# Values of a window attention evacuated flat and spread by DMA instead of by small engine operations

## The reference, in short

```
x = x + window_attention(gn(x))     # 8x8 windows, 16 heads of 16 channels
x = x + lif(gn(x) @ W.T + b)        # leaky integrate and fire over the 8 samples

qkv  = part @ qkv_w.T + qkv_b       # part: (windows, 64 tokens, 256)
attn = softmax(q*SCALE @ k.T + bias_table[...] + shift mask)
out  = attn @ v                     # per window and head: 64x64 times 64x16
```

## Time and profile before

| | |
|---|---|
| median of 3 runs | 576.61 us (572.59 to 577.72) |
| the profiled execution | 574.5 us, its span 572.8 us |
| TensorE (PE) busy | 470.8 us, 82% of the span |
| VectorE (DVE) busy | 464.0 us, 81% |
| ScalarE (ACT) busy | 434.2 us, 76% |
| GpSimd (POOL) busy | 318.1 us, 56% |
| DMA queue of SyncE | 91808 packets, 85.49 MB, 55.8% of 16 DMA engines' span |
| mean granted TensorE clock | 0.951 |

### The profile page before, as it was taken

How to read it: one execution, slowest core, us unless ns; L and a number is a source line. 1 busy time by engine, 2 the same in 40 slices (tenths; PEclk the granted TensorE clock), 3 DMA queues, 4 the chain that set the end, 5 groups by cost and what they waited for, 6 DMA issues and landing times.

```text
span 572.8 us, 18181 instructions
## 1 busy us (share of the span) xinstructions
PE 470.8 (82%) x6632; PEld 426.5 (74%) x6632; DVE 464.0 (81%) x995; ACT 434.2 (76%) x1045; POOL 318.1 (56%) x411
## 2 busy tenths in 40 slices
PE   0364699898999899899989998998999778599880
PEld 0364588787888788788878887887888667599770
DVE  6855568888898789888888987898778775779997
ACT  2275679888898899888888988998889567579830
POOL 6133365566555666655566656566555466867630
PEclk9978799999999999999999999999999898889975
DMA  6266066666777677666667776765565450221233
GB/s 185 73 171 160 15 168 173 175 167 181 190 200 192 165 189 180 165 174 170 181 168 196 193 190 167 186 153 150 155 154 153 132 148 3 92 75 74 97 116 137
DMA packets 92577, 86.09 MB, mean 150 GB/s; under 512 B 41842, under 2 KB 63604, under 8 KB 92532
## 3 DMA queue, kind: packets, MB, share of 16 engines
q1 hardware_dynamic: 91808, 85.49, 55.8%
q10 hardware_dynamic: 724, 0.01, 0.1%
HBM read 47.72 MB, written 33.55 MB: 142 GB/s over the span
## 4 chain that ended last, share of the span: by engine, by line
issue 26%; POOL 24%; PE 21%; DVE 11%; ACT 8%; DMA 6%; SPq 2%; POOLq 1%; ACTq 1%; DVEq 0%
POOL p_lo L426 11%; POOL xc L413 5%; POOL xn_lo L386 3%; DVE xc L865 3%; PE pv_ps L1009 3%; DMA k_stack<-k_spill1lo 2%; ACT v_hi L508 2%; DMA k_spill1lo<-k_lo 2%; PE proj_ps L909 2%; PE proj_ps L911 2%; PE proj_ps L910 2%; PE score_ps L986 2%; DVE charged L857 2%; DMA probs<-in_qkv_b_dram 1%; PE max_ps L953 1%
## 5 line engine op out<-in xcount | busy, mean ns | idle before, releaser
L426 POOL TENSOR_TENSOR p_lo<-probs,p_hi 128x512 f16<-128x512 f32 x128 | 146.7, 1167 | 162.6 <-ACT p_hi L587 162.6
L909 PE MATMUL proj_ps<-xn_hi,w_hi 128*128 128x256 f32 x288 | 86.1, 299 | 14.6 <-POOL xn_lo L386 14.0
L763 DVE TENSOR_TENSOR v_lo<-proj_ps,v_hi 64x128 f16<-64x128 f32 x256 | 74.1, 289 | 22.5 <-ACT v_hi L508 19.8
L586 ACT ACTIVATE probs<-score_ps 128x512 f32<-128x512 f32 x128 | 76.9, 601 | 18.1 <-PE score_ps L986 17.3
L976 PE MATMUL score_ps<-both_parts,bias_k 128*128 128x64 f16 x1024 | 82.6, 194 | 6.2 <-DMA k_stack<-k_spill1lo 4.3
L910 PE MATMUL proj_ps<-xn_lo,w_hi 128*128 128x256 f32 x288 | 83.1, 288 | 0.0
L911 PE MATMUL proj_ps<-xn_hi,w_lo 128*128 128x256 f32 x288 | 83.0, 288 | 0.0
L770 DVE TENSOR_REDUCE neg_max<-max_ps 128x16 f16<-128x1024 f32 x64 | 78.4, 1225 | 4.7 <-PE max_ps L959 2.7
L386 POOL TENSOR_TENSOR xn_lo<-xn,xn_hi 128x512 fp32r<-128x512 f32 x48 | 62.5, 1302 | 34.8 <-ACT xn_hi L480 34.7
L978 PE MATMUL score_ps<-q_stack,k_stack 96*128 96x64 f16 x1024 | 81.8, 193 | 0.0
L472 ACT ACTIVATE xn<-xc,shift,rstd 128x256 f32 (+1 forms) x128 | 70.6, 611 | 12.9 <-DVE shift L238 6.6
(11 more groups left out here) (144 smaller groups left out, 1434.9 us busy)
## 6 DMA issues: line engine op xcount, KB each, us to landing
xc<-in_x_dram SPq DMA_DIRECT2D x32, 256.0 KB, 4.9
k_stack<-k_spill0hi SPq DMA_DIRECT2D x32, 256.0 KB, 4.2
k_stack<-k_spill1hi SPq DMA_DIRECT2D x32, 256.0 KB, 4.1
out_dram<-xc SPq DMA_DIRECT2D x32, 256.0 KB, 2.3
q_hi<-q_flat SPq DMA_DIRECT2D x128, 32.0 KB, 2.0
k_spill0hi<-k_hi SPq DMA_DIRECT2D x16, 256.0 KB, 2.2
k_spill0lo<-k_lo SPq DMA_DIRECT2D x16, 256.0 KB, 2.4
q_stack<-q_spill0hi SPq DMA_DIRECT2D x32, 128.0 KB, 2.8
```

The lines of the kernel that those rows point to most:

```text
L426: pool.tensor_tensor(p_lo[p][:, quads, :, :].rearrange("p g w i -> p (g w i)"), probs[:, quads, :, :].rearrange("p g w i -> p (g w i)"), p ...
L586: act.activation(probs[:, quads, :, :].rearrange("p g w i -> p (g w i)"), score_ps[:, h, :], ACT.Exp)
L909: pe.matmul(dst, w_hi[:, c, cols], high[:, tok], start=(c == 0 and bias is None), stop=False)
```

## The change

The values are copied out of PSUM flat: one operation of 128 x 512 on ScalarE (high part) and one on VectorE (low part), into one tile `v_flat` (partition = token of two windows; part, tile, 256 channels). Four transfers per row, issued by SyncE behind `move_q_and_k`, put them into `v_all`, one for each window and each parity of head: 64 partitions, 4 runs of 256 bytes each. There are two such buffers, zeroed once, with the column of ones set once. For the runs to be contiguous the value columns of the weights are reordered at the start: even heads first, then odd ones, and within them channel by channel with the 8 heads innermost. The part shown for ScalarE's high part of the weights has its like on VectorE for the low part. `weigh_values` now reads its moving operand with a step of 8 elements of 2 bytes between neighbouring columns; before, 34 neighbouring elements were contiguous. `weigh_values` waits for the transfers (`v_moved`), and `v_high` waits until those of the row before have left `v_flat`. The second `v_high` behind `max_rows` is gone. `membrane` shares the space of `q_flat`, which is no longer used by then. Zeroing all value buffers is GpSimd's work now; half of it was VectorE's.

```diff
-        v_hi = [sb(f"v_hi{i}", [128, HALVES, 2, QUADS, 2, D + 1], f16) for i in range(4)]
-        v_lo = [sb(f"v_lo{i}", [128, HALVES, 2, QUADS, 2, D + 1], f16) for i in range(4)]
+        v_flat = sb("v_flat", [128, 2, 2, C], f16)
+        v_all = [sb(f"v_all{i}", [128, 2, 2, 2, 2, D + 1, 2 * QUADS], f16) for i in range(2)]
...
-        membrane = sb("membrane", [128, HALVES * ROWTOK], f32)
+        membrane = q_flat[:, :, :].rearrange("p t n -> p (t n)").bitcast(f32)
...
-        W_SCALES = ((0, C, QK_SCALE), (C, 3 * C, 1.0), (3 * C, OUTS, 1.0 / TAU))
+        W_SCALES = ((0, C, QK_SCALE), (C, 2 * C, 1.0), (3 * C, OUTS, 1.0 / TAU))
...
+        def v_weights(tile, order, c, e):
+            return tile[:, c, 2 * C:3 * C].rearrange(f"p ({order}) -> p e d n", e=2, d=D, n=2 * QUADS)[:, e, :, :]
+        AS_LOADED, BY_PARITY = "n e d", "e d n"
...
+            def move_v(slot, row):
+                sp.wait_ge(v_lo_done, row + 1)
+                for w in range(2):
+                    for e in range(2):
+                        sp.dma_start(v_all[slot][e * WS:(e + 1) * WS, :, :, w, e, 0:D, :].rearrange("j t p d n -> j (t p) (d n)"),
+                                     v_flat[w * WS:(w + 1) * WS, :, :, e * 128:(e + 1) * 128].rearrange("j t p c -> j (t p) c"))\
+                          .then_inc(v_moved[slot], 16)
...
                 if k % 2 == 0 and not is_last_row(row):
                     move_q_and_k((k // 2 + 1) % 2, row + 1, k // 2 + 1)
+                    move_v((k // 2 + 1) % 2, row + 1)
...
-            def v_high(slot, done, w):
+            def v_high(slot, done, moved=0):
                 act.wait_ge(v_ps_done, done)
-                for p in range(2):
-                    for e in range(2):
-                        last = act.activation(v_hi[2 * slot + p][e * WS:(e + 1) * WS, :, w, :, e, 0:D],
-                                              v_part(p, w, e), ACT.Copy)
-                last.then_inc(v_hi_done, 1)
+                wait(act, v_moved[1 - slot], moved)
+                act.activation(v_flat[:, 0, :, :].rearrange("t p c -> t (p c)"), proj_ps[:, 0, :], ACT.Copy).then_inc(v_hi_done, 1)
...
+                if first == C:
+                    for c in range(HALVES):
+                        for e in range(2):
+                            last = act.activation(v_weights(w_hi, BY_PARITY, c, e), v_weights(w_raw, AS_LOADED, c, e), ACT.Copy)
...
-                if p == 1 and not is_last_row(row):
-                    v_high(nxt, row + 2, 1)
...
+            def v_low(done):
+                dve.wait_ge(v_hi_done, done)
+                dve.tensor_tensor(v_flat[:, 1, :, :].rearrange("t p c -> t (p c)"), proj_ps[:, 0, :],
+                                  v_flat[:, 0, :, :].rearrange("t p c -> t (p c)"), ALU.subtract).then_inc(v_lo_done, 1)
...
                 if p == 0:
-                    pe.wait_ge(v_lo_done, row + 1)
+                    pe.wait_ge(v_moved[k // 2], slot_total(row, k // 2, 64))
...
-                        for at, (pp, vv) in enumerate(((p_hi, v_hi), (p_hi, v_lo), (p_lo, v_hi))):
-                            last = pe.matmul(cols[:, :, g, :], pp[p][:, h * QUADS + g, :, :].rearrange("p w i -> p (w i)"),
-                                             vv[k][:, h, :, g, :, :].rearrange("p w e d -> p w (e d)"),
+                        for at, (pp, part) in enumerate(((p_hi, 0), (p_hi, 1), (p_lo, 0))):
+                            last = pe.matmul(cols[:, :, g, :].rearrange("p w (e d) -> p w e d", e=2),
+                                             pp[p][:, h * QUADS + g, :, :].rearrange("p w i -> p (w i)"),
+                                             v_all[k // 2][:, part, p, :, :, :, h * QUADS + g],
                                              start=(at == 0), stop=(at == 2))
```

More of the change, by code:

```diff
@@ L160, in swin_attention_then_lif_kernel @@
         v_lo_done = sem("v_lo_done")
+        v_moved = [sem(f"v_moved{i}") for i in range(2)]
         max_ps_done = sem("max_ps_done")
@@ L265, in swin_attention_then_lif_kernel @@
         ROOT_STEPS = 4 * NEWTONS
-        def v_part(p, w, e):
-            return proj_ps[w * WS:(w + 1) * WS, 0, p * C:(p + 1) * C]\
-                .rearrange("p (h g e d) -> p h g e d", h=HALVES, g=QUADS, e=2)[:, :, :, e, :]
+        def v_weights(tile, order, c, e):
+            return tile[:, c, 2 * C:3 * C].rearrange(f"p ({order}) -> p e d n", e=2, d=D, n=2 * QUADS)[:, e, :, :]
+        AS_LOADED, BY_PARITY = "n e d", "e d n"
         free_averages = proj_ps[:, 0, 0:2 * NORMS]
@@ L320, in move_q_and_k @@
                     stack(part, k_stack[slot], k_spill[slot][src])
-            sp.wait_ge(const_step, 10)
+            def move_v(slot, row):
[5 more added lines that the diff above has]
+                          .then_inc(v_moved[slot], 16)
+            sp.wait_ge(const_step, 9)
             move_q_and_k(0, 0, 0)
+            move_v(0, 0)
             def pair(n, row, k, s):
@@ L362, in _ @@
             pool.memset(q_hi[0][:, :, :, :, :], 0.0)
-            for buf in v_hi[0:2] + v_lo[0:2]:
-                pool.memset(buf[:, :, :, :, :, :], 0.0)
+            for buf in v_all:
+                pool.memset(buf[:, :, :, :, :, :, :], 0.0)
             for buf in max_rows:
@@ L367, in _ @@
             zeroed.then_inc(const_step, 1)
-            def ones_of_values(buffers):
-                for buf in buffers:
-                    for e in range(2):
-                        for h in range(HALVES):
-                            last = pool.memset(buf[e * WS:(e + 1) * WS, h, :, :, e, D:D + 1], 1.0)
-                return last
             pool.wait_ge(const_step, 7)
-            ones_of_values(v_hi[0:2]).then_inc(const_step, 1)
+            for buf in v_all:
+                for e in range(2):
+                    ones = pool.memset(buf[e * WS:(e + 1) * WS, 0, :, :, e, D, :], 1.0)
+            ones.then_inc(const_step, 1)
             pool.wait_ge(const_step, 8)
@@ L389, in _ @@
             low_part(0, 1)
[L390 to L394, removed]
             low_part(1, 2)
@@ L525, in _ @@
             for first, end, scale in W_SCALES:
-                act.activation(w_hi[:, :, first:end], w_raw[:, :, first:end], ACT.Copy, scale=scale).then_inc(setup_act, 1)
+                last = act.activation(w_hi[:, :, first:end], w_raw[:, :, first:end], ACT.Copy, scale=scale)
+                if first == C:
+                    for c in range(HALVES):
+                        for e in range(2):
+                            last = act.activation(v_weights(w_hi, BY_PARITY, c, e), v_weights(w_raw, AS_LOADED, c, e), ACT.Copy)
+                last.then_inc(setup_act, 1)
             act.wait_ge(setup_dve, 3)
@@ L536, in _ @@
             act.wait_ge(const_step, 8)
-            v_high(0, 1, 0)
-            v_high(0, 1, 1)
+            v_high(0, 1)
             xn_high(1, 2)
@@ L541, in _ @@
             bias_high(1)
-            act.wait_ge(const_step, 10)
+            act.wait_ge(const_step, 9)
             def keep_attention(m, p):
@@ L572, in pair @@
                     else:
-                        v_high(nxt, row + 2, 0)
+                        v_high(nxt, row + 2, slot_total(row, k // 2, 64))
                 act.wait_ge(max_turned, n + 1)
@@ L648, in _ @@
                             ident_h[:, 0:16].unsqueeze(2).to_broadcast([128, 16, WS]))
-            for buf in v_hi[2:4] + v_lo[2:4]:
-                dve.memset(buf[:, :, :, :, :, :], 0.0)
             dve.wait_ge(b_loaded, 16 * 7)
@@ L717, in _ @@
                                                 w_hi[:, :, first:end].bitcast(f32), ALU.mult, ALU.subtract)
+                if first == C:
+                    for c in range(HALVES):
+                        for e in range(2):
+                            last = dve.tensor_tensor(v_weights(w_lo, BY_PARITY, c, e), v_weights(w_raw, AS_LOADED, c, e),
+                                                     v_weights(w_hi, BY_PARITY, c, e).bitcast(f32), ALU.subtract)
             last.then_inc(setup_dve, 1)
@@ L793, in _ @@
             dve.wait_ge(const_step, 8)
-            v_low(0, 1)
+            v_low(1)
             maxima(0)
-            dve.wait_ge(const_step, 10)
+            dve.wait_ge(const_step, 9)
             def pair(n, row, k, s):
@@ L811, in pair @@
                     else:
-                        v_low(nxt, row + 2)
+                        v_low(row + 2)
                 if is_first(n, 1):
@@ L856, in lif_units @@
                         dve.wait_ge(reset_done, y * (SAMPLES - 1) + t)
-                        dve.scalar_tensor_tensor(level, membrane[:, :], 1.0 - 1.0 / TAU, banks[t], ALU.mult, ALU.add)\
+                        dve.scalar_tensor_tensor(level, membrane, 1.0 - 1.0 / TAU, banks[t], ALU.mult, ALU.add)\
                            .then_inc(charge_done, 1)
@@ L861, in lif_units @@
                     if t < SAMPLES - 1:
-                        dve.scalar_tensor_tensor(membrane[:, :], level, 1.0, level,
```

(1 more changed line is left out.)

## The result

The changed kernel takes **693.19 us** (median of 4 runs, 691.3 to 696.74) against 577.1 us before: ratio 1.205, 95% interval 1.199 to 1.212. The profiled execution took 691.3 us, its span is 689.5 us. The forecast was 594 us with a range from 558 to 602. The direction was right, the size was not: rival B (pitch 120 to 127 ns, 682 to 693 us) came true, at its upper end.

The account below looks back on a forecast made before the run. TensorE, busy 46.84 of 50 us, was taken to set the pace. 574.5 us, less 12.5 for the evacuation, plus 32.6 for the stepped moving operand, with the transfers and start at 0, gave 594 us, range 558 to 602.

Parts of the forecast that it names:

- rival B: Value matmuls: each 16-byte piece costs its own time, 1.77 to 1.87 ns, pitch 120 to 127 ns, 682 to 693 us; chance 0.12.
- the price of the moving operand: Value matmuls on TensorE: stepped reading raises the pitch from 31 to 59.6 ns, 0.68 us in 48 pairs, +32.6 us.
- the factor: VectorE's stepped against contiguous time an element, 1.77 against 1.04 ns, 1.70; applied to the value matmuls, a pitch of 51 ns.
- the sum's own form: Total under rival B: 62 pairs x 2.13 = 132, less 11.6 for 7 gaps, less 12.5: 574.5 + 108 = 682 us.
- The relief of the evacuation: TensorE's waits at max_rows and the shared bank, pairs with p = 1: 0.52 us less in 24 pairs, -12.5 us.
- rival A: Value matmuls: the step costs TensorE nothing, so only the 12.5 us gain counts, 562 us (558 to 565); chance 0.34.
- The transfers: Four more a row on SyncE, behind the last k_stack: cost 0, the stacks landing at 308.3, wanted at 309.07.
- rival C: SyncE's value transfers hold up the stacks by up to 1.6 us: +40, up to 602 us, down to no change; chance 0.08.
- The gap at the root steps: TensorE's 1.13 us wait for GpSimd's xn_lo, 7 samples: 1.65 us of room takes in 2 x 0.68 us of longer matmuls.
- slower: Whole kernel: chance 0.55 of ending slower than the 571 to 582 us counted as within about 1% of no change.

Follow-up runs that it names:

- e1_flat_contig: Changed kernel, but value matmuls read 68 neighbouring elements instead of steps of 16 bytes (wrong values): 562.84 us, ratio to before 0.974.
- e2_before_step8: Kernel before, but value matmuls read their buffers in steps of 8 elements, 16 bytes (wrong values): 708.98 us, ratio to before 1.230.
- f1_carry_ones: Changed kernel with v_flat rows of 17, the ones carried by the transfers, so value matmuls read contiguous runs: 562.25 us, ratio to before 0.975.
- f2: f1_carry_ones without the four value transfers a row and the waits on them (buffers of ones, wrong values): 558.34 us, ratio to before 0.970.

## Why the prediction was wrong, point by point

**The failed step: the price of the moving operand.** I took a pitch of 59.6 ns between bounds of 31 and 127, "nearest to the factor, since a ratio carries over to another engine better than a time does". It is 121.7 ns. That reason was the mistake: the time carried over, the ratio did not. VectorE's 1.77 ns for each piece and the 1.8 ns measured agree, and TensorE, which at the full clock streams a contiguous column in 0.42 ns, loses far more by such a time than VectorE, which needs 1221 ns for 1024 contiguous elements, 1.2 ns each, anyway. The 0.42 ns are measured in the kernel before: from the start of L953, 512 columns, to the start of L959 are 215 ns, the median of 120 at a granted clock of 1.00 (in the timeline four stretches of 512 columns, from 304.56 to 305.44 us, take 0.88 us); for 68 columns that makes 28.6 ns, where the prediction took 28.3. Its 154 ns and 1.04 ns an element on VectorE are borne out as well: L716 takes 686 ns for 512 elements (groups by shape, kernel before) and 1221 ns for 1024, thus 1.04 ns an element and 151 ns beside them. That both engines meet one and the same cause is argued from this agreement; on VectorE no step but 64 bytes was seen. The float32 projections run close to the same price, with 64 pieces in 120 ns, but are weak evidence: their own streaming, estimated as 256 columns at those 0.42 ns, takes 107 ns of it.

With the measured pitch, the sum's own form gives 62 pairs x 24 x 90.4 ns = 134.5 us, less 7 x 1.65 = 11.6 and less 12.5: 574.5 + 110.4 = 685 us, 6 us short of the 691.3 us measured.

**The 6 us: a term that was missing, and waits that were not counted.** In the two profiled executions, from the start of each matmul to the start of the next, added up by line:

| distances, us | before | changed | difference | in the sum |
|---|---|---|---|---|
| value matmuls | 50.1 | 187.4 | +137.3 | +134.5 |
| score maxima (L953, L959; then L952, L958) | 58.7 | 71.3 | +12.6 | 0 |
| projections of the values (L919 to L921; then L918 to L920) | 52.7 | 56.2 | +3.5 | 0 |
| behind L978, L986 and L1019 (then L977, L985, L1019), where most waits are | 138.5 | 102.9 | -35.6 | -24.1 |
| all matmuls | 542.1 | 658.2 | +116.1 | +110.4 |

The longer value matmuls swallowed more waits than the sum counts, and matmuls whose work is unchanged became slower. For this second part I had no term: it is the clock. In the changed kernel, windows over the block quoted above (307.7 to 310.6) and over what follows it:

```profile
307.70:310.60 2.90, 2.90 (x27) 2.80 (x25) 0.78 (x2) 2.03 (x4) 1.77 (x2) 0.85 0.59 174
310.60:312.90 2.30, 2.30 (x15) 1.75 (x14) 1.57 (x4) 0.00 (x0) 0.50 (x1) 0.50 0.89 269
```

Within the block the granted clock fell from 1.00 to 0.50, and it was 0.50 for the score maxima behind it. TensorE never stood still in the block; its last idle time before the fall is the 0.21 us ahead of L985, at 307.0. The L952 matmuls then start 0.83 us apart, 310.61 to 311.44; in e1_flat_contig, at the full clock, it is 0.43 us (306.53 to 306.96). It does not happen in each pair. In 16 of 64 pairs of the changed kernel this distance lies wholly in a stretch with a granted clock of 0.50, and is 0.83 us; in 46 at 1.00 it is 0.46 us on average. In the kernel before it is 0.78 to 0.84 us in 4 pairs and 0.44 us in 59. The maxima of a pair hold two such distances, so 16 - 4 = 12 more slow pairs x 2 x 0.37 us make 9 us of the 12.6. Over the stretch from 100 to 450 us the mean of such a matmul rose from 378 to 444 ns (the first row is the kernel before, the second the changed one):

```profile
L953 PE MATMUL max_ps<-bias_q,ident_h 128*128 128x512 f16 x104 | 39.3, 378 | 0.0
```

```profile
L952 PE MATMUL max_ps<-bias_q,ident_h 128*128 128x512 f16 x80 | 35.5, 444 | 0.0
```

The windows from 100 to 450 us, in the same order, have a granted clock of 1.00 and 0.95:

```profile
100.00:450.00 350.00, 324.07 (x5075) 291.12 (x5071) 296.22 (x679) 303.30 (x772) 206.04 (x265) 1.00 0.68 176
100.00:450.00 350.00, 345.48 (x3927) 318.14 (x3926) 192.76 (x384) 201.69 (x447) 158.23 (x207) 0.95 0.62 152
```

What the lower clock costs is thus shown by rows at both levels. Why it falls is not: no run holds it fixed, and only that it falls oftener with the long value matmuls is seen (0.95 and, in e2_before_step8, 0.98 from 100 to 450 us, against 1.00 and, in e1_flat_contig, 0.99). Here the fall came behind 2 us of matmuls in flight without a break, at a pitch of 121.7 ns.

**The relief of the evacuation: right in place, partly by luck in size.** -12.5 us was forecast, rival A at 562 us. With the step removed the kernels measure 562.84 (e1) and 562.25 us (f1), 14 to 15 us under the kernel before. Both places are where the prediction put them: the new `v_high` takes 0.60 us and `max_rows` follows at once, and PE's wait for `max_rows` from 100 to 450 us shrinks in f1_carry_ones from the 8.3 us of the earlier trace rows to

```profile
PE score_ps L989 <- ACT max_rows L583: 3.2, 15, 0.2
PE proj_ps L912 <- POOL xn_lo L399: 6.4, 6, 1.1
```

and the 6 waits at the root steps stay, as forecast for a case without the step's price. The parts have other sizes. Ahead of the subtraction of maxima in a pair with p = 1, the last score matmul of the kernel before and then of the changed one, with what follows it:

```profile
302.92 0.19 PE L978 MATMUL score_ps<-q_stack,k_stack 96*128 96x64 f16 x1
303.36 0.62 PE L986 MATMUL score_ps<-max_rows,pick_max 128*128 128x128 f16 x8 [0.25 <-ACT max_rows L575]
315.60 0.19 PE L977 MATMUL score_ps<-q_stack,k_stack 96*128 96x64 f16 x1
315.63 0.61 PE L985 MATMUL score_ps<-max_rows,pick_max 128*128 128x128 f16 x8
```

From start to start 0.44 us became 0.03: 0.41 us won, where the prediction took the idle time of 0.25. Over the profiled executions of the kernel before and e1_flat_contig these distances fell by 9.6 us in all (forecast 6), those at the shared bank by 4.9 us (forecast 6.5). Against that, the distances from the projections of q and k to the next scores, which wait for the stacks, grew by 6.9 us. The prediction put that at nothing, with 0.8 us of cover in the one row it read the earlier trace rows, while TensorE already waited for the stacks 3.4 us in all.

**The transfers: nearly right.** Counted at 0, they cost 3.9 us by the medians of f1 and f2. With the transfers behind the stacks in the queue, TensorE waited 7.3 us for the stacks, and 5.3 us without the transfers; the DMA share in f1_carry_ones, from 300 to 350 us, rose to 0.85 from 0.73, and the value transfers land in 4.0 us in place of 2.2 us in the changed kernel. The 40 us of rival C came in no kernel.

**The gap at the root steps: right in kind.** It was to absorb the longer value matmuls, and the changed kernel shows no such wait any more.

**The chances.** B had 0.12 and "slower" 0.55. VectorE's row, read as a time, deserved more for B than that. Its case against, that float32 "shows only that TensorE needs no more", was sound as far as it goes: by the estimate above, streaming alone takes 107 of the 120 ns. It takes B's second row away, not its first.

## What to carry to other kernels

Before a layout is turned to please a DMA or an evacuation, count the 16-byte pieces that TensorE's moving operand will touch: pieces x 1.8 ns against columns x 0.42 ns (215 ns for 512 columns at a granted clock of 1.00); the larger one is near the pitch, as seen here with 68 float16 columns. If the pieces are the larger one, carry the padding or the ones through the transfer, so that both the transfer and the operand stay contiguous. And where a row of another engine yields a time for one piece of memory, price that time as well as the ratio; here the time was right.

## What the runs showed of the hardware

- Moving operand, 68 float16 columns: pitch 31, 33, 63, 122 and 124 ns at steps of 2, 4, 8, 16 and 32 bytes. With two columns from each 16-byte piece the pitch is 63 ns, twice the 31 ns of contiguous columns.
- The price did not change with TensorE's granted clock. The pitch of contiguous value matmuls did: in f1_carry_ones it is 32.5 ns at a granted clock of 1.00 and 55.5 to 57.5 ns in the four blocks that lie at 0.50. In the changed kernel the blocks that start at 53.12 and at 298.41 us both have a pitch of 122.5 ns (from start to L952 at 56.06 and at 301.35), at granted clocks of 0.61 and 1.00:

```profile
53.10:56.10 3.00, 3.00 (x27) 2.97 (x27) 0.00 (x0) 1.93 (x4) 2.92 (x4) 0.61 0.44 71
298.40:301.30 2.90, 2.90 (x28) 2.76 (x25) 0.00 (x0) 2.05 (x4) 1.75 (x2) 1.00 0.95 176
```

- Loaded operand, 128 float16 columns at 16 bytes (one run): a pitch of 60 ns, a quarter of the moving operand's price a column.
- ScalarE's and VectorE's 128 x 512 evacuations take 600 and 678 ns into rows of 17 elements, against 596 and 683 ns into a flat row:

```profile
L763 DVE TENSOR_TENSOR v_flat<-proj_ps,v_flat 128x512 f16<-128x512 f32 x32 | 21.9, 683 | 14.4 <-ACT v_flat L510 14.4
L510 ACT ACTIVATE v_flat<-proj_ps 128x512 f16<-128x512 f32 x32 | 19.1, 596 | 10.7 <-PE proj_ps L920 10.7
```
